# A four-layer graph network on one core: layer 1's table stored in seven groups, early edge stores and six gathers moved, last parts turned ahead, layer 2's tail in another order

## What is computed

```python
# layer 0: per source node sum, maximum and mean of 32 features of its edges, then an MLP
h = concat([seg_sum, seg_max, seg_mean, u[batch]]); x += relu(h @ W1 + b1) @ W2 + b2
# layer 1: graph attention, 8 heads, with self loops, softmax over the edges of a destination
msg = h[src] * alpha; x += segment_sum(msg, dst).mean(heads) + bias
# layer 2: message MLP and update MLP
m = silu(concat([edge, h[src], h[dst]]) @ W1m + b1m) @ W2m + b2m
x += silu(concat([h, segment_mean(m, dst)]) @ W1u + b1u) @ W2u + b2u
# layer 3: edge weight times cosine similarity of the projected ends
x += scale * (c0 * segment_sum(relu(w*cos)*Wc, row) + c1 * (negative part) + c2 * Wh)
```

## Time and profile before

| | |
|---|---|
| median of 3 runs | 3170.77 us (3169.61 to 3173.38) |
| profiled execution | 3168.2 us, of which the span 3166.4 |
| busy: TensorE | 643.9 us (20%) |
| busy: VectorE | 1318.1 us (42%) |
| busy: ScalarE | 496.7 us (16%) |
| busy: GpSimd | 2202.2 us (70%) |
| mean granted clock of TensorE | 0.576 |

### The profile page before, as it was taken

One profiled execution on the slowest core, in us unless ns is written; L12 is line 12 of the kernel. 1 busy time (PEld: TensorE's weight loads), 2 busy tenths in 40 slices (PEclk: granted clock), 3 DMA queues, 4 the chain that ended last, 5 costly groups with the idle time before them and its releaser, 6 DMA issues. The chain is left out here.

```text
span 3166.4 us, 14581 instructions
## 1 busy us (share of the span) xinstructions
PE 643.9 (20%) x3384; PEld 477.8 (15%) x3385; DVE 1318.1 (42%) x1864; ACT 496.7 (16%) x463; POOL 2202.2 (70%) x2299
## 2 busy tenths in 40 slices
PE   5421130002410000001888850001000600000001
PEld 5411110001300000001567630000000400000001
DVE  8888875102210000008466642242435405353455
ACT  2200007111100000001100122232323211221220
POOL 0177777777677777777777767777776367777774
PEclk8765565555555555555899975555555555555555
DMA  9211124212355766654355424333332132323231
GB/s 330 97 25 14 14 27 110 51 33 64 78 50 54 62 61 59 64 56 58 80 136 150 111 51 81 98 108 108 92 124 80 21 63 72 89 72 90 72 90 48
DMA packets 195122, 248.82 MB, mean 79 GB/s; under 512 B 138380, under 2 KB 149229, under 8 KB 187510
## 3 DMA queue, kind: packets, MB, share of 16 engines
q0 software_dynamic: 74048, 114.24, 19.7%
q1 hardware_dynamic: 62950, 104.45, 10.3%
q10 hardware_dynamic: 58064, 29.51, 8.2%
HBM read 154.12 MB, written 93.93 MB: 78 GB/s over the span
## 5 line engine op out<-in xcount | busy, mean ns | idle before, releaser
L808 POOL DMA_INDIRECT l0g_rows<-in_rec_s,ents x440 | 427.8, 972 | 138.5 <-issue 133.8
L763 POOL DMA_INDIRECT l1g_rows<-tab,srct x440 | 416.2, 946 | 144.5 <-issue 133.8
L763 POOL DMA_INDIRECT l2g_rows<-tab,ep_rows x440 | 416.1, 946 | 134.1 <-issue 134.1
L763 POOL DMA_INDIRECT l3g_rows<-tab,others x440 | 415.2, 944 | 134.1 <-issue 134.1
L1268 POOL DMA_INDIRECT ep_rows<-recp,entd x352 | 348.9, 991 | 107.3 <-issue 107.3
L1465 DVE TENSOR_TENSOR l1s_A<-l1s_A,l1s_mk 110x4096 f32<-110x4096 f32 x1 | 4.4, 4422 | 539.9 <-ACT l1s_A L1442 539.9
L1720 PE MATMUL l1a_pa<-l1a_g,l1a_wt 128*128 x1296 | 168.8, 290 | 0.0
L1720 PEld LDWEIGHTS l1a_pa<-l1a_g,l1a_wt 128*128 128x128 f32 x1296 | 158.3, 202 | 24.1 <-issue 24.1
L2250 DVE COPY l2g_mix<-l2g_q 128x64 f32<-128x64 f32 x12 | 2.7, 228 | 318.2 <-ACT l2g_mix L2221 318.2
L2596 DVE COPY l3g_filled<-l3g_q 128x65 f32<-128x65 f32 x12 | 2.7, 228 | 310.9 <-ACT l3g_filled L2565 310.9
L2657 PE MATMUL l3t_nmp<-ident,l3t_nmb 128*64 128x128 f32 x2 | 0.7, 448 | 583.6 <-DVEq L2674 583.6
(11 more groups left out here) (566 smaller groups left out, 2446.8 us busy)
## 6 DMA issues: line engine op xcount, KB each, us to landing
l1a_g<-g SPq DMA_DIRECT2D x54, 390.0 KB
recp<-ep_rows ACTq DMA_DIRECT2D x11, 1320.0 KB, 5.7
g<-l1g_rows ACTq DMA_DIRECT2D x10, 1430.0 KB, 25.3
sums<-l0s_sums SPq DMA_DIRECT2D x10, 1408.0 KB
sums<-l2o_sums SPq DMA_DIRECT2D x9, 1408.0 KB
sums<-l3o_sums SPq DMA_DIRECT2D x9, 1408.0 KB, 5.4
rowsd<-ep_rows POOLq DMA_DIRECT2D x8, 1452.0 KB, 5.8
ep_rows<-rowsd SPq DMA_DIRECT2D x8, 1452.0 KB, 6.6
```

The source lines that it names most:

```text
L763: nc.gpsimd.indirect_dma_start(out=ring.rows[:, s, j, :], out_offset=None, in_=table, in_offset=bass.IndirectOffsetOnAxis(ap=index(b, s, j ...
L808: nc.gpsimd.indirect_dma_start(out=rows[:, j, :], out_offset=None, in_=K.a["rec_s"], in_offset=bass.IndirectOffsetOnAxis(ap=K.by_src.ent[: ...
```

## The change

- The first sort has 15 units ahead of the first turn instead of 20; the other 40 are spread over the seven stretches.
- LEFT = 6: only 60 edge gathers follow `l0f_res` before the meeting, and none of the two block stores. The store of block 2 becomes the first thing that GpSimd issues in layer 1's gather. The six gathers that are left, and behind ten gathers of the next block the store of block 3, go into `remaining_edges`.
- Layer 1's table is stored by SyncE in seven pieces, each as soon as its group is computed; the step of `node_dense` now is the meeting of all engines, and `store_table` goes.
- In the gathers of layers 2 and 3, part 10 (SIDE) gets PSUM banks of its own (`pair`, `beside`). ScalarE turns part 10 before it waits for part 9's sums, and part 11 (in the first banks) before it waits for part 10's.
- In layer 2's tail the carries get two banks of their own. Two lots (16 products) are computed ahead of the pipeline, the other two (8 and 1) in rounds 2 and 4. VectorE normalises group t - 3 in round t, ahead of the join of group t - 1; the loop has one more round.

```diff
@@ -51,6 +51,7 @@
+LEFT = 6
@@ -60,6 +61,8 @@
+SIDE = NBLK
+CARRY_AT = (2, 4)
@@ -562,7 +565,7 @@
-AHEAD = 20
+AHEAD = 15
@@ -1025,6 +1028,11 @@
+                if send is not None:
+                    for t, (w, n) in enumerate(groups):
+                        sp.wait_ge(used, t + 1)
+                        send(sp, slice(w, w + n))
+                    sp.wait_ge(stored, 16 * n_groups)
@@ -1139,7 +1147,7 @@
         collect(K, K.by_src, K.sums0, D // 2, res, True)
-        early_edges(K, RING * TB + EARLY, RING * TB - EARLY)
+        early_edges(K, RING * TB + EARLY, RING * TB - EARLY - LEFT)
         half = D // 2
@@ -1197,19 +1205,12 @@
-        node_dense(K, "t1m", K.hn, D, None, 2 * H, None, None, None, put, w1d=V, pool_ahead=True)
-        store_table(K, K.tab1, tab)
...
-def store_table(K, table, tab, pool_ahead=False):
-    nc = K.nc
-    with Phase(K, "st" + table.tensor.name) as ph:
-        stored = ph.sem("stored")
-        with Step(nc, pool_ahead) as block:
-            @block.sync
-            def _(sp):
-                sp.dma_start(table.rearrange("(w p) r -> p w r", p=P), tab[:, :, :]).then_inc(stored, 16)
-                sp.wait_ge(stored, 16)
...
+        tab1_stored = ph.sem("tab1_stored")
...
+        def send(sp, ws):
+            sp.dma_start(K.tab1.rearrange("(w p) r -> p w r", p=P)[:, ws, :], tab[:, ws, :]).then_inc(tab1_stored, 16)
+        node_dense(K, "t1m", K.hn, D, None, 2 * H, None, None, None, put, w1d=V, send=send, stored=tab1_stored)
@@ -1247,9 +1248,6 @@
-            for s in range(RING):
-                if first + n == 2 * RING * TB:
-                    store_edges(K, nc, pool, slice((RING + s) * TB, (RING + s + 1) * TB), s, TB * 16)
@@ -1273,8 +1271,13 @@
+            for c in range(2 * RING * TB - LEFT, 2 * RING * TB):
+                nc.gpsimd.indirect_dma_start(
+                    out=ring.rows[:, 1, c % TB, :], out_offset=None, in_=K.recp,
+                    in_offset=bass.IndirectOffsetOnAxis(ap=K.by_dst.ent[:, c:c + 1], axis=0)
+                ).then_inc(ring.gathered[1], 16)
...
-                gather(it * RING, it, 0, (it - 1, 1) if it > 2 else None)
+                gather(it * RING, it, 0, (it - 1, 1))
@@ -1352,6 +1355,7 @@
+            store_edges(K, nc, pool, slice(RING * TB, (RING + 1) * TB), 0, TB * 16)
             gather_blocks(nc, pool, ring, K.tab1, lambda b, s, j: K.srct[:, b * TB + j:b * TB + j + 1], ready)
@@ -2125,7 +2129,8 @@
-        turn, own = ph.ps("turn"), ph.ps("own")
+        pair = ph.ps("pair", (P, 2 * 512))
+        turn, own = pair[:, 0:512], pair[:, 512:]
@@ -2147,6 +2152,9 @@
+        def bank_of(i):
+            return pair if i == SIDE else mix_banks
@@ -2210,20 +2218,31 @@
+                def turn_rows(i):
+                    b, c0, n, landed, count = parts[i]
+                    act.wait_ge(landed, count)
+                    if i == SIDE:
+                        act.wait_ge(moved, 2 * NG)
+                    elif i > SIDE:
+                        act.wait_ge(packed, SIDE)
+                    elif i:
+                        act.wait_ge(packed, i)
+                    nc.scalar.copy(cut(bank_of(i), n)[:, :, 1:],
+                                   ring.rows[:, b % RING, c0:c0 + n, D:].rearrange("p j f -> p f j")).then_inc(spread, 1)
...
-                    s = b % RING
-                    mix = cut(mix_banks, n)
-                    act.wait_ge(landed, count)
-                    if i:
-                        act.wait_ge(packed, i)
-                    nc.scalar.copy(mix[:, :, 1:], ring.rows[:, s, c0:c0 + n, D:].rearrange("p j f -> p f j")).then_inc(spread, 1)
+                    mix = cut(bank_of(i), n)
+                    if i < SIDE:
+                        turn_rows(i)
...
+                    if SIDE <= i + 1 < len(parts):
+                        turn_rows(i + 1)
@@ -2302,7 +2321,7 @@
-        carry_banks = (pa[0], pa[1], pb[0], pb[1])
+        carry_banks = [ph.ps(f"carried{i}") for i in range(2)]
@@ -2330,13 +2349,20 @@
-                for w in range(NT):
-                    lt = nc.tensor.matmul(carry_banks[w // 8][:, w % 8 * D:(w % 8 + 1) * D], sel[:, w * P:(w + 1) * P], car[:, :],
-                                          start=True, stop=True)
-                    if w % 8 == 7 or w == NT - 1:
-                        lt.then_inc(carry, 1)
-                pe.wait_ge(kept, 4)
...
+                def carries(i):
+                    if i >= 2:
+                        pe.wait_ge(kept, i - 1)
+                    for w in range(8 * i, min(8 * i + 8, NT)):
+                        lt = nc.tensor.matmul(carry_banks[i % 2][:, w % 8 * D:(w % 8 + 1) * D], sel[:, w * P:(w + 1) * P], car[:, :],
+                                              start=True, stop=True)
+                    lt.then_inc(carry, 1)
...
+                carries(0)
+                carries(1)
...
+                    if t in CARRY_AT:
+                        carries(2 + CARRY_AT.index(t))
@@ -2384,11 +2410,17 @@
-                for i, bank in enumerate(carry_banks):
+                def keep_carries(i):
...
-                    nc.scalar.copy(carried[:, w:w + n, :], bank[:, 0:n * D].rearrange("p (w d) -> p w d", d=D)).then_inc(kept, 1)
+                    nc.scalar.copy(carried[:, w:w + n, :],
+                                   carry_banks[i % 2][:, 0:n * D].rearrange("p (w d) -> p w d", d=D)).then_inc(kept, 1)
...
+                keep_carries(0)
+                keep_carries(1)
...
+                    if t in CARRY_AT:
+                        keep_carries(2 + CARRY_AT.index(t))
@@ -2437,7 +2469,7 @@
-                for t in range(NG + 2):
+                for t in range(NG + 3):
@@ -2446,15 +2478,8 @@
                         v.tensor_tensor(res[:, ws, :], res[:, ws, :], wide(T.r, ws, n), ALU.mult).then_inc(averaged, 1)
-                    if 1 <= t <= NG:
-                        u = t - 1
-                        w, n = GROUPS[u]
-                        dve.wait_ge(first, u + 1)
-                        if u >= 2:
-                            dve.wait_ge(acted, u - 1)
-                        v.tensor_tensor(both[:, u % 2, 0:n * P], pb[u % 2][0:D, 0:n * P], T.own[0:D, w * P:(w + n) * P], ALU.add).then_inc(joined, 1)
-                    if t >= 2:
-                        u = t - 2
+                    if t >= 3:
+                        u = t - 3
                         w, n = GROUPS[u]
@@ -2469,6 +2494,13 @@
+                    if 1 <= t <= NG:
+                        u = t - 1
+                        w, n = GROUPS[u]
+                        dve.wait_ge(first, u + 1)
+                        if u >= 2:
+                            dve.wait_ge(acted, u - 1)
+                        v.tensor_tensor(both[:, u % 2, 0:n * P], pb[u % 2][0:D, 0:n * P], T.own[0:D, w * P:(w + n) * P], ALU.add).then_inc(joined, 1)
```

33 lines of the change are left out of this document (22 added, 11 removed).

## The result

The changed kernel took 3137.02 us (median, 3135.87 to 3139.58), the kernel before beside it 3170.19 us (3168.59 to 3173.38). The ratio is 0.9895 with a 95% interval of 0.9878 to 0.9912: 33.2 us less, where 36.1 was forecast. The profiled execution of the changed kernel took 3139.6 us (span 3137.8), the longest of its runs, and that of before 3168.2, shorter than all four of its runs. So the two traces show only 28.6 us of the 33.2, and what follows accounts for those 28.6.

A forecast was written before the change was run, and what follows sets the result against it. GpSimd's back-to-back gathers bound the kernel, so only its waits and the first sort could give time: 6.4 + 8.8 + 3.0 + 12.8 + 5.1 = 36.1 us, from 3170.8 to 3134.7, range 3125 to 3144.

The forecast's parts named there:

- first sort: Ahead of layer 0's gathers: VectorE's 7.20 us wait at the first turn falls to about 0.6; minus 6.4 us.
- 82 early gathers: Gathers ahead of layer 1's meeting: everything up to the meeting shifts as one with the sort; no further change, 0.
- meeting, to layer 1's first gather: Layer 1's first meeting: still 10.71 us, now behind a gather instead of block stores; first gather 9.8 us earlier.
- from there to layer 2's start: Layer 1: GpSimd carries six gathers and a store later, is last by 0.7 us; minus 8.8 taken after 9.8.
- end of layer 2's gather: Part 11 starts when its rows land, at 2441.3 instead of 2444.37; minus 3.0 us.
- layer 2's tail: VectorE normalises earlier groups while TensorE works, so TensorE needn't stand; variance at 2505.7 instead of 2518.53, minus 12.8 us.
- end of layer 3's gather: VectorE's waits for the turns of parts 10 and 11, 3.21 and 2.07 us, go; minus 5.1 us.
- rival (b): Layer 1's meeting was dear because of bulk stores, cheap behind gathers: minus 16 instead of 8.8, 3127.5 us; chance 0.08.
- rival (e): Gathers' ends: ScalarE's copy beside VectorE's PSUM scan slows both, 2 us each end, 3139; chance 0.17 shared with (c).
- Rival (a): Layer 2's tail: TensorE's clock rises from 0.50 as it is busy nearly always; 3 us, 3131.7; chance 0.10.
- (d): Layer 1's sums: TensorE's clock granted later, 0.31 us per slower matmul; with 200 more, 3197 us; chance 0.03.
- Rival (c): Six-unit sort stretches or layer 2's rounds give part back: half 3139.3, all 3144 us; chance 0.17 shared with (e).

The follow-up runs named there:

- the two tail runs below 3170 us: The kernel before with only VectorE's order in layer 2's tail changed, 3153.09 us; the kernel before with only the carries changed, 3166.56 us.

## Right and wrong, step by step

| step | forecast | in the two traces |
|---|---|---|
| first sort | 6.4 | 3.4 |
| 82 early gathers | 0 | -2.2 |
| meeting, to layer 1's first gather | 9.8 | 9.3 |
| from there to layer 2's start | -1.0 | -2.7 |
| layer 2's gathers | 0 | -1.0 |
| end of layer 2's gather | 3.0 | 3.0 |
| layer 2's tail | 12.8 | 14.9 |
| end of layer 3's gather | 5.1 | 4.2 |
| collecting gathers of layer 3 | 0 | -0.4 |
| sum | 36.1 | 28.5 |

**First sort: the mechanism right, the size off by half.** The forecast allowed 0.2 us for stretches of six units and priced only ScalarE's copies. The term missed the staging slots: a batch is five units, so a sixth unit in a stretch begins a new batch and needs the slot whose store isn't yet there. The store issued at 64.57 landed 15.3 us later. The gain of 3.4 lay within the bounds given, 2.1 to 6.6. The new wait varies: 3.76, 2.05, 2.07, 2.08 and 1.32 us in the five traces with the changed sort, 0.56 and 0.57 in the two with the stretch before the fourth turn at five.

**The meeting: right.** GpSimd's time from its last gather to its next DMA is 11.01 us against 10.71 taken, and the rival (b), cheap behind gathers, fell. The group stores stayed covered. The row for six of them (KB each, us to landing), and SyncE issuing all seven:

```profile
tab<-t_tab SPq DMA_DIRECT2D x6, 164.0 KB, 3.2
...
826.49 14.30 SPq L1212 DMA_DIRECT2D tab<-t_tab  x7
```

The last is issued at 840.8 and lands 3.2 us later, at 844, some 13 us before it is wanted. At 164 KB in 3.2 us a store moves 51 KB/us, against 91 for the one of 1,025 KB. The Trainium skill, DMA: Bandwidth & Descriptors, section Measured, wants transfers of at least 1 MiB; by the rate the trace agrees, and the time didn't depend on it here. The rule and the fixed 2 us that the forecast's estimate took from that page of the Trainium skill are given there for DMAs that GpSimd issues, and these stores are SyncE's: a store took 3.2 us where the estimate made it 3.6.

That GpSimd's own time bounds the meeting was argued in the forecast from the end of the kernel. At the end it is now shown by the run that leaves the drain out. At the meeting the traces show it: the table had landed at 844, and GpSimd's drain ended at 855.5, 2.2 us ahead of the next DMA. What the meeting costs without it, no run on such a chip shows.

**GpSimd's queue behind it: the step that failed.** The forecast had GpSimd last at layer 2 by 0.7 us and the start 15.2 earlier with the sort's share (6.4 + 8.8). It was last, as said, by 1.5 us, but the start came only 7.8 earlier. Of the 7.4 missing, 3.0 are the sort's; 2.2 the early gathers', which took 701.2 us from the first of layer 0 to the 82nd before and 703.4 now; 0.5 the stretch to layer 1's first gather (9.3 for 9.8); and 1.7 the stretch from there to layer 2 (2.7 given back for 1.0). The last is the queue: the moved store waited 2.3 us for the rows of block 3, and some tenths elsewhere went the other way. The forecast priced that store at its issue and named no wait. Without the wait the start would still have come only 1.5 us earlier, since the table was ready no sooner: its chain took 1.2 us longer than before from layer 1's first gather on, which the forecast had at nothing. What made it longer isn't shown.

The early gathers' slowing shows in their mean, 1022 ns for the 82 against 999 for the 88 of before. The longest in both traces lie over one of VectorE's operations on 1600 columns: in the changed kernel one of 2.42 us at 805.62 over an operation of 1.83 us at 805.39; over the same operation, at 809.48, the longest took 1.79 us before. That the sort's shift moved the gathers against these operations is my reading. In the two tail runs below 3170 us, which have the old sort, the same stretch took 701.0 and 699.1 us, so a part of it may be chance.

**Layer 2's tail: right, with the reason in the right place.** TensorE's 33.7 us from the second group on and the 1 us of hand-overs came out as 34.3 together (2456.73 to 2490.99), the remainder as 3.1. Of the 14.9, 14.6 lie ahead of the variance, 1.8 more than forecast, and 1.45 of these are the start: the second group's rows arrived 12.3 us behind the first collecting gather instead of 13.8. The forecast's working was too kind to the carries, whose spreading gains nothing measurable; it put their 4.05 us on TensorE's path and they are there, but they had not been in the way before. The earlier start is not the edit's either: with the order alone the second group's rows arrived at 13.5 us, and the variance came at 50.9 all the same.

**Ends of the gathers: right.** Layer 2's 3.0 exactly. Layer 3's 4.2 of 5.1: 0.4 of waits that never go to zero, 0.35 for two small steps of part 9, of which only one (0.16) lies beside ScalarE's copy, so that rival (e) came at most at a twelfth of its price in that end and not at all in the other, and 0.4 because part 9 began that much later behind the gathers (the waits themselves were 5.3). Rival (a) fell (clock 0.50), and (d) did not come. Rival (c) came true by half: the sort's stretches gave back some 3 us, while TensorE's rounds in layer 2 kept no wait. The rest of what is missing, ahead of layer 2, stood in no rival.

**The total.** That the medians come within 2.9 us of the forecast is luck in part: between the two traces it misses by 7.6, and the tail's 2.1 beyond its forecast hides as much again of what other terms lost. 33.2 by the medians lies between the 28.6 of the traces and the forecast; which term is larger in the other executions than in the profiled one, no trace shows. Layer 3's table is one candidate: from its last store's issue to its landing it took some 7 us in the traces of before and of the change and some 4.5 in the two of the tail's parts.

## What to carry to other kernels

A step moved out of a wait keeps its cost on the engine that issues it, and it also brings its own waits along: price the semaphore that it waits for at its new place, not only its issue (2.3 us of wait here, of which 1.5 counted). Where a pipeline engine (here VectorE) both feeds and drains another, put the draining of an older item ahead of the feeding's wait; that alone was worth 15 us here, and spreading the work that was thought to be in the way was worth nothing. A wait that reads 0.3 us after a change doesn't mean that the start is as early as it can be: look who is last now.

## What the runs showed of the hardware

At a meeting behind its own DMAs GpSimd's drain ended 8.8 us behind a gather, 8.5 behind a 1,452 KB store, and 9.3 behind the last gather at the kernel's end. The next DMA stood at 11.0 and 10.7 us, the end of the span at 9.5 and 9.6, of which 4.7 went when the last meeting exchanged semaphores without drains.

The same program took 3170 us on some chips and 3981 to 3987 on others. On the latter the instructions last as long on VectorE and ScalarE (1316.4 and 497.4 us busy, 1318.1 and 496.7 on the former), but beneath GpSimd's gathers and for some microseconds behind them hand-overs between engines, and of VectorE to itself, arrived 1 to 11 us late in the rows shown, and a quarter of the gathers had a pitch of 1.40 instead of 1.25 us. The whole change gained 33.2 us on the first kind and 28.2 on the second; its part that removes short waits at the gathers' ends (3.0 and 4.2 us in the traces of the first) gained nothing on the second.
